# An attention stack on one core: values of two key tiles in one block, maxima moved ahead of it

## What is computed

```
q, k, v = heads(x_norm @ Wq + bq), heads(ctx @ Wk + bk), heads(ctx @ Wv + bv)
w = softmax(q k^T * 8**-0.5, axis=-1)        # 256 x 1601 (cross) or 256 x 256 (self), 16 heads
x = x + gate * ((w @ v) @ Wp + bp)           # for each of 16 elements
```

## Time and profile before

| | |
|---|---|
| runs | 6714.82, 6722.88, 6731.32 us |
| profiled execution | 6733.98 us, span 6732.2 us |
| mean granted TensorE clock | 0.967 of full speed |
| TensorE matmul busy | 6088.2 us (90%) |
| VectorE busy | 4124.3 us (61%) |
| ScalarE busy | 4247.2 us (63%) |
| GpSimd busy | 985.3 us (15%) |
| maxima, line 1074 | 6144 products, 1582.8 us |
| scores, line 1058 | 11008 products, 2097.0 us |
| values, line 1104 | 22016 products, 1769.7 us |

### The profile page before, as it was taken

How to read it: one execution, slowest core, us unless ns; L and a number is a source line. 1 busy time by engine, 2 the same in 40 slices (tenths; PEclk the granted TensorE clock), 3 DMA queues, 4 the chain that set the end, 5 groups by cost and what they waited for, 6 DMA issues and landing times.

```text
span 6732.2 us, 147754 instructions
## 1 busy us (share of the span) xinstructions
PE 6088.2 (90%) x49714; PEld 3143.3 (47%) x49714; DVE 4124.3 (61%) x6520; ACT 4247.2 (63%) x8158; POOL 985.3 (15%) x1660
## 2 busy tenths in 40 slices
PE   6999999999777999999999677699999999979998
PEld 3444444444444444444444344344444444435554
DVE  5767777776555666666666255467777776624332
ACT  3777777777665776776677366477777777732222
POOL 3112112211111111111110011122112211100000
PEclk9999999999998999999999899899999999989998
DMA  2222222221112222222231011222232222101110
GB/s 85 75 69 62 63 76 66 56 74 43 58 58 71 78 68 56 76 70 57 71 78 35 17 57 57 64 67 64 68 78 68 56 75 76 38 32 41 42 43 23
DMA packets 181115, 405.58 MB, mean 60 GB/s; under 512 B 16992, under 2 KB 124560, under 8 KB 166416
## 3 DMA queue, kind: packets, MB, share of 16 engines
q1 hardware_dynamic: 180752, 400.01, 22.1%
HBM read 316.81 MB, written 83.14 MB: 59 GB/s over the span
## 4 chain that ended last, share of the span: by engine, by line
PE 73%; issue 8%; DVE 8%; ACT 7%; DMA 2%; SPq 1%; POOL 1%; ACTq 0%; DVEq 0%; POOLq 0%
PE bank L1058 18%; PE bank L1104 18%; PE pair L1074 14%; DVE MX L1400 3%; PE bank L1030 2%; ACT P L1234 2%; PE bank L645 2%; PE bank L1025 2%; PE bank L636 2%; PE pair L1091 1%; DMA QP<-scr_q 1%; PE pair L1080 1%; ACT QP L1245 1%; PE pair L574 1%; DVE ST L1357 1%
## 5 line engine op out<-in xcount | busy, mean ns | idle before, releaser
L1234 ACT ACTIVATE P<-bank 128x512 f32<-128x512 f32 (+1 forms) x5504 | 3104.0, 597 | 1415.4 <-PE bank L1058 1375.1
L1400 DVE TENSOR_REDUCE MX<-pair 128x2 f32<-128x802 f32 x3072 | 2923.9, 988 | 1367.4 <-PE pair L1074 1359.8
L1058 PE MATMUL bank<-QP,KP 128*128 128x256 bf16 (+1 forms) x11008 | 2097.0, 277 | 155.3 <-ACT P L1234 100.2
L1104 PE MATMUL bank<-P,VA 128*25 128x256 f32 (+1 forms) x22016 | 1769.7, 392 | 38.2 <-issue 32.8
L1074 PE MATMUL pair<-KP,QP 96*128 96x401 bf16 x6144 | 1582.8, 339 | 60.3 <-DMA QP<-scr_q 42.0
L1058 PEld LDWEIGHTS bank<-QP,KP 128*128 128x128 bf16 (+1 forms) x11008 | 859.3, 100 | 1598.6 <-ACT P L1234 917.4
L1104 PEld LDWEIGHTS bank<-P,VA 128*25 128x25 f32 (+1 forms) x22016 | 403.6, 102 | 751.7 <-issue 497.2
L1074 PEld LDWEIGHTS pair<-KP,QP 96*128 96x128 bf16 x6144 | 595.3, 99 | 184.1 <-DVE MX L1400 64.0
L1404 DVE TENSOR_REDUCE MX<-pair 128x4 f32<-128x1024 f32 x256 | 311.3, 1223 | 327.2 <-PE pair L1080 326.5
L1525 POOL COPY VA<-VN 128x416 f32<-128x416 f32 (+1 forms) x320 | 139.2, 436 | 2533.6 <-PE bank L1104 2452.1
L1245 ACT CAST QP<-pair 2x512 bf16<-2x512 f32 x640 | 339.5, 576 | 130.1 <-PE pair L1091 124.6
(11 more groups left out here) (213 smaller groups left out, 4611.1 us busy)
## 6 DMA issues: line engine op xcount, KB each, us to landing
KP<-scr_k SPq DMA_DIRECT2D x192, 900.6 KB
QP<-scr_q SPq DMA_DIRECT2D x960, 48.0 KB
CN<-ctx_n SPq DMA_DIRECT2D x40, 768.0 KB
scr_k<-KSF SPq DMA_DIRECT2D x48, 600.8 KB, 3.2
scr_k<-KSF SPq DMA_DIRECT2D x48, 600.0 KB, 3.2
CT<-ctx_t SPq DMA_DIRECT2D x24, 800.5 KB, 4.5
KP<-scr_ks SPq DMA_DIRECT2D x128, 144.0 KB
scr_q<-QS SPq DMA_DIRECT2D x80, 192.0 KB, 2.1
```

The costliest lines, as they stand in the source:

```text
L1058: last = nc.tensor.matmul(SC[half][0:kt, k * N:(k + 1) * N], KP[g][:, c0:c0 + kt], QP[g][:, h * N:(h + 1) * N], start=True, stop=True)
L1104: last = nc.tensor.matmul(OB[32 * h:32 * h + STEP + HD + 1, 0:N], VA[g % 2][0:kt, t, h, :], P[(g * ph.nt + t) % 2][0:kt, h * N:(h + 1) * N ...
L1234: nc.scalar.activation(P[v % 2][0:kt, half * 2 * N:(half + 1) * 2 * N], SC[half][0:kt, :], ACT.Exp, scale=SCALE).then_inc(sem("probs_full" ...
L1400: nc.vector.tensor_reduce(MX[:, r, c:c + 2], MP[j % 2][:, :].rearrange("p (t k) -> p t k", t=2)[:, :, 0:SPANS[0][1]], AX.X, ALU.max).then_ ...
```

## The change

The probabilities get four buffers in place of two. TensorE no longer does the values of one tile in every slot. In every slot with an odd number v it does the values of two tiles, v - 3 and v - 2, in one block between the score halves. In cross phases the maxima follow the parity of v: two in an even slot (one between the halves, one after the second half) and one in an odd slot, after the second half. In self phases the maxima keep their places (both in tile 0). The pieces d, e and y of a self phase go from slots 1, 3, 4 to slots 2, 4, 5. ScalarE's copies of the head sums go from tile 0 to tile 1 of their group. The counts of the semaphores are moved to fit.

```diff
--- before.py
+++ after.py
@@ -23,6 +23,7 @@
 NG = H // G
 NPAIR = NG // 2
 STEP = 16
+NP = 4
 R9 = 9 * HD
 MR = 96
 SCALE = float(HD) ** -0.5
@@ -138,9 +139,12 @@
     def after(self):
         return self.c.after()
 
-    def maximum_at(self, slot):
+    def maximum_at(self, slot, odd):
 
         t, n = slot
+        if self.cross and n > NG:
+            first = [sum(2 - (i + odd) % 2 for i in range(k)) for k in range(n - 1)]
+            return list(range(first[t], min(first[t + 1], self.nm))) if t < n - 2 else []
         spread = max(n - 2, 1)
         return [j for j in range(self.nm) if min(j * spread // self.nm, n - 1) == t]
 
@@ -176,7 +180,7 @@
                 pieces += [(0, "post", n) for n in ("d", "e", "y")]
         else:
             if prev:
-                at = dict(d=3, e=5, y=9) if ph.cross else dict(d=1, e=3, y=4)
+                at = dict(d=3, e=5, y=9) if ph.cross else dict(d=2, e=4, y=5)
                 pieces += [(at[n], "post", n) for n in at]
             if nxt:
                 pieces += nxt[0].prep_slots(ph)
@@ -271,7 +275,7 @@
     ALU, ACT, AX = mybir.AluOpType, mybir.ActivationFunctionType, mybir.AxisListType
     ds = bass.ds
 
-    start = dict(probs_full=3, pv_done=2, heads_copied=2, mlp_centered=1, mlp_gated=1)
+    start = dict(probs_full=3, pv_done=NP, heads_copied=2, mlp_centered=1, mlp_gated=1)
     start["misc_full"] = 0
     names = {}
     plan = []
@@ -316,7 +320,7 @@
         QP = [sb("QP%d" % g, [128, G * N], bf16) for g in range(NG)]
         VA = [sb("VA%d" % k, [128, len(CROSS_TILES), G, STEP + HD + 1], f32) for k in range(2)]
         VN = sb("VN", [128, len(CROSS_TILES), D], f32)
-        P = [sb("P%d" % k, [128, G * N], f32) for k in range(2)]
+        P = [sb("P%d" % k, [128, G * N], f32) for k in range(NP)]
         CN = sb("CN", [128, len(CROSS_TILES), D], f32)
         CT = sb("CT", [D, len(CROSS_TILES) * 128], f32)
         KSF = sb("KSF", [D, 3 * S + 1], bf16)
@@ -1102,32 +1106,33 @@
                 pe.wait_ge(sem("probs_full"), at("probs_full", b, 2 * (g * ph.nt + t + 1)))
                 for h in range(G):
                     last = nc.tensor.matmul(OB[32 * h:32 * h + STEP + HD + 1, 0:N], VA[g % 2][0:kt, t, h, :],
-                                            P[(g * ph.nt + t) % 2][0:kt, h * N:(h + 1) * N],
+                                            P[(g * ph.nt + t) % NP][0:kt, h * N:(h + 1) * N],
                                             start=(g % 2 == 0 and t == 0), stop=(g % 2 == 1 and t == ph.nt - 1))
                 last.then_inc(sem("pv_done"), 1)
 
             def element(el):
                 ph, b = el.ph, el.b
-                last_tile = (el.prev[0], el.prev[1], NG - 1, el.prev[0].nt - 1) if el.prev else None
+                held = [(el.prev[0], el.prev[1], NG - 1, el.prev[0].nt - k) for k in (2, 1)] if el.prev else []
                 for g in range(NG):
                     ahead = (ph, b, g + 1) if g + 1 < NG else (*el.nxt, 0) if el.nxt else None
                     for t in range(ph.nt):
-                        js = ahead[0].maximum_at((t, ph.nt)) if ahead else []
-                        third = -(-len(js) // 3)
+                        odd = (g * ph.nt + t) % 2
+                        js = ahead[0].maximum_at((t, ph.nt), g % 2) if ahead else []
+                        early = 0 if odd and ph.cross else -(-len(js) // 3)
                         among, behind = el.here(g * ph.nt + t)
                         scores(ph, b, g, t, 0)
-                        for j in js[:third]:
+                        for j in js[:early]:
                             maximum(*ahead, j)
+                        if len(held) == 3:
+                            for tile in held[:2]:
+                                head_values(*tile)
+                            held = held[2:]
                         for piece_ in among:
                             piece(el, *piece_)
                         scores(ph, b, g, t, 1)
-                        for j in js[third:2 * third]:
+                        for j in js[early:]:
                             maximum(*ahead, j)
-                        if last_tile:
-                            head_values(*last_tile)
-                        last_tile = (ph, b, g, t)
-                        for j in js[2 * third:]:
-                            maximum(*ahead, j)
+                        held.append((ph, b, g, t))
                         if ahead and t == ph.shift_tile:
                             shift_rows(*ahead)
                         for piece_ in behind:
@@ -1156,7 +1161,8 @@
                         element(ph.el["middle"](i))
                     element(ph.el["last"])
                     if ph.el["after"]:
-                        head_values(ph, B - 1, NG - 1, ph.nt - 1)
+                        for t in range(ph.nt - 2, ph.nt):
+                            head_values(ph, B - 1, NG - 1, t)
                         for piece_ in sum(ph.el["after"].here(0), []):
                             piece(ph.el["after"], *piece_)
                 elif isinstance(ph, MlpPhase):
@@ -1230,8 +1236,8 @@
                 at, kt, v = ph.c.at, ph.tiles[t], g * ph.nt + t
                 act.wait_ge(sem("scores_full"), at("scores_full", b, 2 * v + half + 1))
                 if half == 0:
-                    act.wait_ge(sem("pv_done"), at("pv_done", b, v - 1))
-                nc.scalar.activation(P[v % 2][0:kt, half * 2 * N:(half + 1) * 2 * N], SC[half][0:kt, :], ACT.Exp,
+                    act.wait_ge(sem("pv_done"), at("pv_done", b, v + 1 - NP))
+                nc.scalar.activation(P[v % NP][0:kt, half * 2 * N:(half + 1) * 2 * N], SC[half][0:kt, :], ACT.Exp,
                                      scale=SCALE).then_inc(sem("probs_full"), 1)
 
             def copy_heads(ph, b, p):
@@ -1259,11 +1265,11 @@
                         if ph.cross:
                             for piece_ in among:
                                 piece(el, *piece_)
-                        if t == 0 and g == 2:
+                        if t == 1 and g == 2:
                             if el.prev:
                                 act.wait_ge(sem("misc_free"), el.use("post", "e") + 1)
                             copy_heads(ph, b, 0)
-                        elif t == 0 and g == 0 and el.prev:
+                        elif t == 1 and g == 0 and el.prev:
                             copy_heads(*el.prev, 1)
                         if ahead and t == ph.shift_tile:
                             copy_rows(*ahead)
@@ -1300,7 +1306,7 @@
             nc.vector.memset(VN[:, FULL, :], 0.0)
             nc.vector.memset(OB[:, :], 0.0).then_inc(sem("cleared"), 1)
 
-            for name, n in (("probs_full", 3), ("pv_done", 2), ("heads_copied", 2)):
+            for name, n in (("probs_full", 3), ("pv_done", NP), ("heads_copied", 2)):
                 dve.sem_inc(sem(name), n)
             for name in ("mlp_centered", "mlp_gated", "l_centered"):
                 dve.sem_inc(sem(name), 1)
@@ -1423,7 +1429,7 @@
                     ahead = (ph, b, g + 1) if g + 1 < NG else (*el.nxt, 0) if el.nxt else None
                     for t in range(ph.nt):
                         among, behind = el.here(g * ph.nt + t)
-                        mine = ahead[0].maximum_at((t, ph.nt)) if ahead else []
+                        mine = ahead[0].maximum_at((t, ph.nt), g % 2) if ahead else []
                         third = -(-len(mine) // 3)
                         for j in mine[:third]:
                             maximum(*ahead, j)
```

## The result

The kernel after takes 7174.58 us (median of four runs, 7150.20 to 7191.35) against 6726.41 (6714.82 to 6731.32) beside it: 1.0666 times, interval 1.063 to 1.0702. I had forecast slower, at 6978 with a range of 6850 to 7110. The direction was right; 197 us were missing, and the time lies 65 us above the range.

A forecast was written before the change was run, and what follows sets the result against it. TensorE was taken to bound the middle of a group, a chain through VectorE and ScalarE its end. 6733.98 us + 230 (cross phases) + 26 (self phases) = 6990, given as 6978 by the runs' median; range 6850 to 7110.

The forecast's parts named there:

- The blocks: Cross phases, values of two tiles together: 1.11 us against 1.32 for two visits, 5.5 us an element saved.
- The maxima: Cross phases, two alternating buffers: a maximum waits for a reduction, so a slot pair takes 3.49 us against 3.25.
- So c waits 0.46 us: Cross phases: the third maximum comes 1.13 us after the first, whose buffer is free only after 1.59; it waits 0.46.
- The group ends and group 0: Cross phases: middles and ends of groups cost about +3 us an element net; group 0 adds +1.5 or about +2.
- The cross elements as a whole: Phases a0, c1 and c2: +4.8 us an element of each kind, 48 elements, +230 us; bounds +2.5 and +8 an element.
- Self phases: 32 elements of s1 and s2, waiting for packed loads: later q projection and more clock falls, +26 us, bounds -70 and +50.
- Sum +26: Total for s1 and s2 in us: q 0.3 later in each of 32 elements, plus 16 for clock falls.
- If two in three do: Elements of s1 and s2 where TensorE's clock falls to 1.2 GHz, before one in three or four: 16 us more.
- POOL, DMA, edges: Whole kernel: buffers, packing and head copies costed at nothing; TensorE's issue stalls -50 to +30 us, taken as 0.
- A moved instruction order may hit or miss that: -50 to +30, taken as 0: TensorE's 15 issue stalls, mostly in slot 1 of c1's elements, 5 to 6 us each: no net change costed.
- the clock falls at the group ends: Rival: in cross phases one in three of 192 group ends loses some 2 us to TensorE's clock: +128, 7106; chance 0.12.
- The rivals in which blocks pay: Cross phases: buffer waits don't bind, -262 us, 6461, chance 0.06; half the waits, group ends free, 6583, chance 0.04.

The follow-up runs named there:

- experiment 9: Kernel before with 256 idle waits (128 instructions) on TensorE between phases a0 and s1, moving the later loops: 6668.58 us, 0.9904.
- experiment 10: Kernel after with 64 idle TensorE waits ahead of the phases and 208 between a0 and s1, moving its loops: 6985.31 us, 1.0374.
- experiment 6: Kernel after with its self phases s1 and s2 as in the kernel before, cross phases unchanged: 7116.64 us, 1.0577.
- experiment 4: Kernel after with 64 idle waits (32 instructions) on TensorE ahead of the first phase: 7076.28 us, 1.0518.
- Experiment 3: Kernel after with the maxima placed as in the kernel before: 7027.12 us, 1.0445.
- Experiment 7: Kernel before with 256 idle waits (128 instructions) on TensorE ahead of the first phase: 6719.28 us, 0.9985.
- experiment 2: Kernel before with SyncE loading the next context first and group 3's packs only after slot 7 of the next element: 6669.87 us, 0.9914.
- experiment 1: Kernel after with SyncE loading the next context first and group 3's packs only after slot 7 of the next element: 7068.14 us, 1.0499.

## Why the prediction was right or wrong

Right, by its own steps:

- *The blocks.* 16 products take 0.99 us to the next start, forecast 1.02. At the blocks the Trainium skill's rule (TensorEngine Tiling (Array Packing), Key Properties) holds, since fewer entries save time; by itself it gave the wrong sign for the kernel.
- *The maxima.* "So c waits 0.46 us", a pair of 3.49: measured 0.47 and 3.49. Forecast were some 11 waits an element; the view has 548 waits over 48 elements, 11.4.
- *The group ends and group 0.* Before the row matmuls TensorE is idle for 0.98 us at the end of group 3 in most elements; at the end of group 1 it is 1.54 in c1, but only 0.16 and 0.35 in a0 and c2 (forecast 1.2 for both groups). That is 80 us together, and most of the rest of the 142.6 us stands at the end of group 0, where 36 stood before. Piece q waits up to 1.1 us for ON, 45 times (forecast 1.2).
- *The cross elements as a whole.* With stalls out of the way (experiments 9 and 10) they cost +4.5 in a0, +6.4 in c1 and +4.9 in c2, mean 5.3; forecast +4.8. c1 is the one that was too low. It has one projection fewer to cover a wait; whether that is the reason was not tested.

Off in size:

- *Self phases*, "Sum +26": elements 1 to 14 of s1 and s2 cost 44 us more, in experiment 6 against the kernel after and in experiment 10 against 9 alike. The step that failed is "If two in three do": in the kernel after and in experiment 10 the clock falls to 1.2 GHz in every one of the 28 elements, in stretches of 3.4 or 6.8 us, once in the elements of 28.1 us and twice in most of those of 29.6 and 31.0. In s1 and s2 of experiment 9 (the kernel before) the elements without such a fall last 26.8, those with 3.4 us of it 27.3, those with 6.8 us 28.5. Experiment 10 has 102 us more at the lower level than experiment 9, so by these prices some 15 to 26 of the 44 us are the clock, by my estimate. The rest is 0.6 to 1.0 us an element, where I had q 0.3 later.

Wrong:

- *POOL, DMA, edges*, the step "A moved instruction order may hit or miss that: -50 to +30, taken as 0". What these stalls cost grew by 131 us. Putting the loops in a place where they fetch nothing takes 7174.58 - 6985.31 = 189 us off the kernel after (experiment 10) and 6726.41 - 6668.58 = 58 off the kernel before (experiment 9); by the ratios, which go by the runs beside each, it is 196 and 65. The padding costs 14 and 12 us of its own in them. I had seen the stall and bounded it by what 15 of them cost before. But only 8 of c1's 14 elements had a stall of over 1 us, and none of a0's and c2's. In c2 the fetches fell 3.7 and 0.3 us ahead of the element's start and 8.6 us after it, the burst from 0 to +9 us. In the kernel after they fall, in the element shown, at -3.2, +4.9 and +10.9, the burst from -1 to +8. One of them is now well inside, and 12 of c2's 14 elements stall. a0, which fetched nothing before, fetches 9 packets an element, because its loop starts 16 instructions earlier; experiment 4 moves it 32 instructions later, and it fetches 0 again. The upper bound should have been every cross element stalling: 5 to 6 us each as I had it, over the 40 elements that did not stall before some 220. That price was low as well: a stalled element of c1 lasts 100.4 to 101.4 us against 93.5 in experiment 9. A price known from one phase was not carried to the others.

The rival "the clock falls at the group ends" was given 128 us. In experiment 10 the clock falls once, for 3.4 us, in 2 to 4 elements of 14 in a cross phase, at the end of group 0 or 1, and these are 1.3 to 1.6 us longer than the rest: 8 elements, some 12 us in all, with a granted clock of 1.00 over each phase. The rivals in which blocks pay fell with the 3.49. Experiment 3 adds what none of them had: with the buffer waits gone, ScalarE is next, for a half behind a block has its exponential too late, and the pair is 3.39.

The sum of experiment 10 (6985) lies near my number (6978) partly by chance: the kernel before, freed of its own stalls, runs at 6669, so the order alone costs 317 us and not 256. The 197 us that I missed are thus 131 of stalls and some 61 of order, the rest being the difference between runs of the kernel before. Of the 317, the elements 1 to 14 of the cross phases hold 221, those of the self phases 44, and the rest lies in first and last elements and was not taken apart.

## What to carry to other kernels

Where two buffers alternate, spacing counts and not number: three maxima packed into 1.13 us against a buffer's turnaround of 1.59 lose more than the saved entries bring, and a saving in an engine's switches should be set against the distance from each buffer's use to its next. In a long hardware loop an issue wait without a semaphore deserves a count of the instruction queue's packets in each iteration, and a bound for all phases that could have it. Any edit that adds or removes instructions ahead of a loop can move such a stall, so a change should be compared with both versions free of it. Here 128 idle instructions between two phases made the kernel before 1% faster, without touching the work.

## What the runs showed of the hardware

- **A loop of TensorE of some 120 KB fetched nothing or 9 packets an iteration, by its place alone.** By my count of addresses, loops that lie within eight blocks of 16 KB had 0 fetches from the third element on (but for a single packet in the last iteration of some), and those that touch a ninth had 9. Experiment 7 swapped a0 and c1 in this. Where the blocks begin is not in the count. It is fitted: with one and the same offset (53 to 68 instructions all do) the rule gives all 42 cross loops of the 14 kernels right. The Trainium skill (Runtime: NRT & Kernel Launch, Instruction fetch mechanics) gives TensorE 128 KiB, refilled in 16 KiB blocks, which agrees with eight blocks. It also says that a taken branch to a target outside the current two-page window forces a fetch before execution goes on; the 0 fetches of experiment 9, in loops of over seven such blocks, do not agree with that. What the engine keeps inside was not measured, only the packets.
- **A fetch that meets a burst of data is late by microseconds.** In the stalled elements of c1 in the kernel before, the second fetch comes at +4.1 to +5.0 us, and at +0.3 with the burst moved (experiment 2); in c2 of the kernel after at up to +5.2 against +0.3 to +1.0 (experiment 1). The stalls behind it are up to 4.1 and 4.8 us. In c2 of the kernel before, where the fetches fell just ahead of the burst and near its end, 9 packets an iteration cost nothing visible (97.5 us, and 97.5 with none in experiment 9). The stall of some 2 us at the start of an element stays without the burst and goes with the fetches (experiment 10); what makes it is open.
- **A stall costs twice.** Behind it TensorE's clock is down to 1.2 GHz (0.61 against 0.39 for two score products): in c2 of the kernel after 4.3 us an element of issue waits stand beside a granted clock of 0.97, some 7 us an element at the lower level. The element is 7.2 us longer than in experiment 10 (109.5 against 102.3).
